# Attention logits and their transposes in two 64-row halves of the array, two quads of heads at a time

## The chip, the cores and the metric

The kernel runs on one core of a Trainium2 chip. The metric is the device time of one execution in microseconds (us); lower is better. Shorthand: PE is TensorE, DVE VectorE, ACT ScalarE, POOL GpSimd, SP SyncE. L476 is line 476 of the kernel.

## The reference

For 16 batches of 128 tokens with 256 features: a layer norm, cross attention with 32 heads of 8 features and axial rotary positions, a residual, a second layer norm, and a mixture of 32 experts (6 per token) with a shared expert. The change is in the attention:

```python
q = (x @ Wq).reshape(b, n, 32, 8)
k, v = jnp.split(ctx @ Wkv, 2, axis=-1)      # each reshaped to (b, ctx_n, 32, 8)
q, k = apply_axial_rope(q, pos), apply_axial_rope(k, pos)
logits = jnp.einsum('bqhd,bkhd->bhqk', q, k) * scale
w = jax.nn.softmax(logits, axis=-1)
attn = jnp.einsum('bhqk,bkhd->bqhd', w, v).reshape(b, n, 256)
x = x + attn @ Wout + bout
```

## The kernel before

Attention runs first, then the mixture. In attention the 32 heads of a batch are 8 quads of 4; each head has a slot of 32 partitions in the array, 24 of them holding its 8 features as fp16 high and low parts, and row 24 (`MAXROW`) the negated row maximum. `qst` is q transposed, [128 slots' rows, quad, 128 tokens]; `kz` is k transposed, spread over four blocks j such that block j is zero outside slot j, [128, 4, quad, 128 keys].

For each quad the logits are computed twice. `logits_q` (L568, matmul L576) computes S for a quad in one matmul of 512 columns (four heads of 128 keys) into `SB[u % 2]`; DVE's `row_max` (L472) reduces it to four maxima per token in `mx` (L476). For every two quads ("half" 0 to 3) PE transposes `mx` into a corner of `SB[1]` (`transpose_max`, L578), DVE copies it to `mxs` (`evac_max`, L479, L483), and SP sends it to row `MAXROW` of `qst` (L295). Then `logits_k` (L582, L589) computes S^T minus the maximum, four matmuls of 128 columns, into `STB[g % 2]`; ACT takes the exponential (L369) into `pw[g % 4]`, in fp32. `weigh_values` (L593, L600) multiplies by V in four column strips of 32 and accumulates in `OB`; one such call is a quad, 8 matmuls in the trace.

SB and STB are two PSUM banks each. S^T of quad g waits for exponential g - 2 (`at_least(pe, exp_ok, QUADS * m.n + g - 1)`), S of quad u for reduction u - 2, and for odd u also for the copy of the maxima (`mxs_ok`). The exponential of quad g waits for `weigh_values` of quad g - 4, since `pw` has four buffers.

The order is written out by hand. Each engine runs `period(b)` for b = -3 to 16 with eight steps g = 0 to 7, and each handles several batches at once: b (the current one), m1 = b + 1, m2, m3, m4 ahead and o = b - 1 behind. All queues are in order. On PE (L626): at each g `logits_k(b, g)`; at odd g `transpose_max`; at each g `logits_q` of quad g + 5 of b (g < 3) or g - 3 of m1. Besides, g = 0: `project_v(m1)` (L566), `weigh_values(o, 4..7)`, `transpose_xc(m3)` (L538, L539); g = 1: `transpose_q(m1)` (L554), `project_k(m3)` (L543); g = 2: `project_q(m3)` (L547); g = 3: `transpose_outputs(o)` (L608); g = 4: `weigh_values(b, 0..3)`, `transpose_attn(o)` (L615); g = 5: `transpose_k(m2)` (L561), which waits for DVE's rotation (L469) to have left its bank; g = 6: `project_out(o)` (L621).

ACT (L363) has the exponential first at each g, and then g = 0: copies to V (L374, which waits for all of `weigh_values(o)`) and xcT (L359); g = 1: qst (L380); g = 2: OT (L407); g = 4: the norm of m4 (L353); g = 5: attnT (L397); g = 6: kT (L402). DVE (L495) has at g = 3 the rotation by cos (`rope_cos`, L462), the copy of maxima (L483), a reduction, and `normalise(o)` (L489 reciprocal, L492 product); at g = 4 a reduction and the rotation by sin (L469, two instructions); at g = 7 the residual (L501), the copy of maxima, a reduction and statistics (L514). SP (L279) sends kT to kz in four DMAs at the start of a period once all exponentials of the batch before are done, and the maxima at odd g. POOL splits q and k into fp16 parts (`split`, L247 to L260) after the rotation.

Of the kernel before, what the change touches and what calls it, by code (L numbers as in the profile page):

```python
# [157 lines left out]
def attention(nc, sem, X, identf, st2, ring, ahead, x, ctx_in, pos, wq, wkv, wout, bout):  # L158
    with ExitStack() as es:
# [181 lines left out]
        def _(act):  # L341
# [21 lines left out]
            def period(b):  # L363
                m1, m2, m3, m4, o = b + 1, b + 2, b + 3, b + 4, b + -1
                for g in range(QUADS):
                    if inside(b):
                        act.wait_ge(st_mm, QUADS * b.n + g + 1)
                        at_least(act, pv_mm, QUADS * b.n + g - 3)
                        act.activation(pw[g % 4][:, :], STB[g % 2][:, :], ACT.Exp, scale=SCALE).then_inc(exp_ok, 1)  # L369
# [7 lines left out]
                    if g == 1 and inside(m1):  # L377
                            at_least(act, qstT_mm, m1.n + 1)
                            at_least(act, st_mm, QUADS * b.n)
# [32 lines left out]
        def _(dve):  # L412
# [59 lines left out]
            def row_max(m, u):  # L472
                dve.wait_ge(s_mm, QUADS * m.n + u + 1)
                if not (isinstance(m.n, int) and 4 * m.n + u // 2 < 2):
                    dve.wait_ge(mxT_mm, 4 * m.n + u // 2 - 1)
                dve.tensor_reduce(mx[u // 2 % 2][:, u % 2:8:2], SB[u % 2][:, :].rearrange("p (j t) -> p j t", j=4),  # L476
                                  axis=AX.X, op=ALU.max, negate=True).then_inc(max_ok, 1)
# [17 lines left out]
            def period(b):  # L495
                m1, m3, o = b + 1, b + 3, b + -1
                for g in range(QUADS):
# [10 lines left out]
                    who, u = (b, g + 5) if g < 3 else (m1, g - 3)  # L508
                    if inside(who):
                        row_max(who, u)  # L510
# [18 lines left out]
        def _(pe):  # L529
# [38 lines left out]
            def logits_q(m, u):  # L568

                if u == 0:  # L570
                    at_least(pe, qst_ok, m.n + 1)
                    pe.wait_ge(kz_in[m.par], 64 * (m.half + 1))
                at_least(pe, max_ok, QUADS * m.n + u - 1)
                if u % 2:
                    at_least(pe, mxs_ok, 4 * m.n + u // 2)
                pe.matmul(SB[u % 2][:, :], qst[m.par][:, u, :], kz[m.par][:, :, u, :], start=True, stop=True).then_inc(s_mm, 1)  # L576
# [5 lines left out]
            def logits_k(m, g):  # L582

                at_least(pe, exp_ok, QUADS * m.n + g - 1)
                if g % 2 == 0:
                    half = g // 2
                    pe.wait_ge(mr_in[half % 2], 16 * (2 * m.n + half // 2 + 1))
                for j in range(4):
                    ins = pe.matmul(STB[g % 2][:, j * P:j * P + P], kz[m.par][:, j, g, :], qst[m.par][:, g, :],  # L589
                                    start=True, stop=True)  # L590
# [710 lines left out]
```

## Time and profile before

| | us |
|---|---|
| median of 3 runs | 429.85 (429.79 to 432.39) |
| the profiled execution, its own time | 428.33 |
| its span, first to last instruction | 426.6 |
| mean granted TensorE clock | 0.911 |
| PE busy | 317.8 (74%) |
| DVE busy | 236.8 (55%) |
| ACT busy | 201.3 (47%) |
| POOL busy | 167.3 (39%) |

Times of instructions come from the one profiled execution. A matmul is in work from its start to its modelled end, and the next one starts before that end; the distance between starts is what a matmul takes of the engine in a stream. Attention runs until about 237 us, the mixture from there.

### The profile page before, as it was taken

To read this page: it belongs to the slowest core of one execution; us is meant where nothing else is said; L and a number is where in the kernel's file an instruction comes from. 1 tells how busy PE (TensorE), PEld (TensorE's weight loads), DVE (VectorE), ACT (ScalarE), POOL (GpSimd) and SP (SyncE) were. 2 spreads that over 40 slices of the span, in tenths; PEclk is the share of its full clock that TensorE was granted. 3 is DMA by queue.
4 is the path that set the end of the run, shared out by engine and by line. 5 is a ranking of instruction groups with operands and counts; after the bars stand their busy time and mean duration, and the time that the engine had idled before them with its cause. 6 is when DMAs were issued, how large, how long until landed. Compare 5 with 4: busy or idle time off the path is not lost. (4 is left out here: it accounts for less than half of the span.)

```text
span 426.6 us, 9168 instructions
## 1 busy us (share of the span) xinstructions
PE 317.8 (74%) x2986; PEld 212.4 (50%) x2986; DVE 236.8 (55%) x624; ACT 201.3 (47%) x378; POOL 167.3 (39%) x241
## 2 busy tenths in 40 slices
PE   0473878999999999999986588797988996775000
PEld 0251646777777777777664234454566543331000
DVE  6464447677777777777774457999682321221000
ACT  2232456776777777776774663535724121110000
POOL 9342144233344444443000200443785225776720
PEclk9997689999999999999999589999999999996555
DMA  7898276211111111103200235110336694222255
GB/s 191 252 256 238 55 211 193 55 35 31 31 32 32 31 32 25 31 23 91 62 18 2 75 125 206 25 51 1 101 102 206 198 245 109 28 26 26 28 94 111
DMA packets 35035, 39.27 MB, mean 92 GB/s; under 512 B 8032, under 2 KB 29120, under 8 KB 34752
## 3 DMA queue, kind: packets, MB, share of 16 engines
q1 hardware_dynamic: 24082, 21.55, 17.6%
q10 hardware_dynamic: 8030, 11.93, 9.7%
q0 software_dynamic: 2896, 5.44, 7.4%
q8 instruction: 15, 0.25, 0.3%
q14 instruction: 12, 0.10, 0.1%
HBM read 26.36 MB, written 10.32 MB: 86 GB/s over the span
## 5 line engine op out<-in xcount | busy, mean ns | idle before, releaser
L476 DVE TENSOR_REDUCE mx<-bank 128x4 f16<-128x512 f32 x128 | 87.2, 684 | 30.0 <-PE bank L576 29.9
L369 ACT ACTIVATE pw<-bank 128x512 f32<-128x512 f32 x128 | 76.8, 601 | 52.0 <-PE bank L600 31.0
L247 POOL TENSOR_TENSOR rot<-t 128x256 f32<-128x256 f32 x30 | 21.1, 726 | 108.1 <-DVE t L469 108.1
L576 PE MATMUL bank<-kz,qst 128*128 128x512 f16 x128 | 51.1, 400 | 7.2 <-DMA kz<-kT 5.9
L589 PE MATMUL bank<-qst,kz 128*128 128x128 f16 x512 | 50.7, 223 | 6.5 <-DMA qst<-mxs 5.9
L589 PEld LDWEIGHTS bank<-qst,kz 128*128 128x128 f16 x512 | 38.3, 100 | 19.4 <-issue 7.5
L600 PE MATMUL bank<-pw,V 128*32 128x128 f32 x1024 | 34.7, 276 | 0.0
L877 POOL DMA_INDIRECT out<-ac,dst x16 | 21.7, 1354 | 28.6 <-DVE ac L1118 10.4
L1118 DVE TENSOR_SCALAR ac<-mbank,wpair 128x256 f32<-128x256 f32 x16 | 7.7, 484 | 44.0 <-DMA odd<-ac,dst 41.2
L1175 PE MATMUL mbank<-hT,WSG 128*128 128x512 f16 (+1 forms) x144 | 32.0, 379 | 0.0
L600 PEld LDWEIGHTS bank<-pw,V 128*32 128x32 f32 x1024 | 25.9, 109 | 8.8 <-issue 7.5
L1187 PE MATMUL mbank<-WSD,ac 128*128 128x256 f32 (+1 forms) x96 | 23.8, 404 | 6.5 <-POOL ac L836 4.0
L836 POOL TENSOR_TENSOR ac<-ac,sg 128x512 f32<-128x512 f32 (+1 forms) x9 | 11.8, 1319 | 39.9 <-ACT ac L917 39.9
L483 DVE COPY mxs<-bank 8x128 f16<-8x128 f16 x64 | 13.1, 205 | 22.4 <-PE bank L580 22.4
L1187 PEld LDWEIGHTS mbank<-WSD,ac 128*128 128x128 f32 (+1 forms) x96 | 19.1, 202 | 11.3 <-POOL ac L836 6.5
L877 POOL DMA_INDIRECT odd<-ac,dst x16 | 21.7, 1354 | 7.4 <-DVE ac L1118 5.3
L402 ACT COPY kT<-bank 128x1024 f16<-128x1024 f16 x16 | 16.1, 1008 | 14.6 <-PE bank L561 12.5
L1175 PEld LDWEIGHTS mbank<-hT,WSG 128*128 128x128 f16 (+1 forms) x144 | 15.1, 106 | 15.4 <-ACT ac L917 0.4
L258 POOL TENSOR_TENSOR tokst<-rot,tokst 128x256 f16<-128x256 f32 x30 | 20.1, 671 | 4.4
L538 PE MATMUL bank<-identf,xn 128*128 128x128 f32 x32 | 7.9, 333 | 15.8 <-ACT xn L353 13.9
L1244 PE MATMUL mbank<-ring_gu,xbT 128*64 128x352 f32 x112 | 18.9, 460 | 0.7 <-ACT xbT L778 0.7
L970 ACT ACTIVATE ac<-mbank 128x176 f32<-128x176 f32 x16 | 5.1, 318 | 29.7 <-PE mbank L1244 29.7
(175 smaller groups left out, 645.9 us busy)
## 6 DMA issues: line engine op xcount, KB each, us to landing
ring_gu<-in_L_ffn_w_gate_up ACTq DMA_DIRECT2D x20, 352.0 KB
kz<-kT SPq DMA_DIRECT2D x64, 64.0 KB, 2.0
ring_dn<-in_L_ffn_w_down ACTq DMA_DIRECT2D x10, 352.0 KB
ring_gu<-in_L_ffn_w_gate_up SPq DMA_DIRECT2D x8, 352.0 KB
X<-in_x SPq DMA_DIRECT2D x4, 512.0 KB, 7.4
table<-ac SPq DMA_DIRECT2D x8, 256.0 KB, 2.1
odd<-zero SPq DMA_DIRECT2D x1, 2048.0 KB, 7.2
out<-X SPq DMA_DIRECT2D x4, 512.0 KB, 3.3
```

The lines of the kernel that those rows point to most:

```text
L247: eng.tensor_tensor(rot[:, part], t1[:, part], t2[:, part], ALU.add).then_inc(rot_ok[w], 1)
L258: eng.tensor_tensor(tokst[m.par][:, w, :, a:a + HD], r, hi, ALU.subtract)
L369: act.activation(pw[g % 4][:, :], STB[g % 2][:, :], ACT.Exp, scale=SCALE).then_inc(exp_ok, 1)
L402: act.copy(kT[:, :, :], M1[:, :].bitcast(F16).rearrange("p (q t) -> p q t", q=QUADS)).then_inc(kT_ok, 1)
L476: dve.tensor_reduce(mx[u // 2 % 2][:, u % 2:8:2], SB[u % 2][:, :].rearrange("p (j t) -> p j t", j=4), axis=AX.X, op=ALU.max, negate=True). ...
L576: pe.matmul(SB[u % 2][:, :], qst[m.par][:, u, :], kz[m.par][:, :, u, :], start=True, stop=True).then_inc(s_mm, 1)
L589: ins = pe.matmul(STB[g % 2][:, j * P:j * P + P], kz[m.par][:, j, g, :], qst[m.par][:, g, :], start=True, stop=True)
L600: ins = pe.matmul(OB[m.par][32 * j:32 * j + 32, (g % 4) * P:(g % 4) * P + P], V[m.par][:, a:a + SLOT], pw[g % 4][:, j * P:j * P + P], star ...
L877: pool.indirect_dma_start(to[:, :], bass.IndirectOffsetOnAxis(ap=dst[:, 2 * k + w:2 * k + w + 1], axis=0), ys[k % 3][rows, :], None, compu ...
L1175: ins = pe.matmul(GU[2 * (i % 2) + w][0:n, :], WSG[:, c, u, w * SHARED + a:w * SHARED + a + n], hT[:, v, c, 512 * k:512 * k + 512], start= ...
L1187: ins = pe.matmul(DN[m % 2][:, 0:D], ac[k % 2][0:n, f, j * P:j * P + P], WSD[0:n, f, :], start=(f == 0), stop=(f == 2))
L1244: ins = pe.matmul(EB[k % 3][lane, 0:2 * INNER], xbT[:, c, e * CAP:e * CAP + LANE], ring.gu[place][:, e % 2, c, :], start=(c == 0), stop=(c ...
```

## The change

S and S^T go by pairs of quads p = 0 to 3. Rows 0 to 63 of the array hold slots 0 and 1 of a quad, rows 64 to 127 slots 2 and 3. The upper half (r = 0) writes `SB[0]` or `STB[0]`, the lower half `SB[1]` or `STB[1]`, each for both quads (a = 0, 1) of the pair. `logits_q(m, p)` is four matmuls of 256 columns on 64 rows in place of two of 512 on 128 rows; `logits_k(m, p)` is eight matmuls of 128 columns on 64 rows in place of eight on 128. `row_max(m, p)` is two reductions, one for each bank; the exponentials are two for each pair as before, one for each bank. A bank pair is written when both of its last readers are done. PE runs `logits_k` and `logits_q` at even g only, and `transpose_max` at the end of odd g.

```diff
--- before.py
+++ after.py
@@ -364,9 +364,10 @@
                 m1, m2, m3, m4, o = b + 1, b + 2, b + 3, b + 4, b + -1
                 for g in range(QUADS):
                     if inside(b):
-                        act.wait_ge(st_mm, QUADS * b.n + g + 1)
-                        at_least(act, pv_mm, QUADS * b.n + g - 3)
-                        act.activation(pw[g % 4][:, :], STB[g % 2][:, :], ACT.Exp, scale=SCALE).then_inc(exp_ok, 1)
+                        r = g % 2
+                        act.wait_ge(st_mm, 4 * b.n + g // 2 + 1)
+                        at_least(act, pv_mm, QUADS * b.n + g - r - 2)
+                        act.activation(pw[g % 4][:, :], STB[r][:, :], ACT.Exp, scale=SCALE).then_inc(exp_ok, 1)
                     if g == 0 and inside(m1):
                         at_least(act, v_mm, m1.n + 1)
                         act.wait_ge(consts, 6)
@@ -376,7 +377,7 @@
                         evac_xcT(m3)
                     if g == 1 and inside(m1):
                             at_least(act, qstT_mm, m1.n + 1)
-                            at_least(act, st_mm, QUADS * b.n)
+                            at_least(act, st_mm, 4 * b.n)
                             act.copy(qst[m1.par][:, :, :], M0[:, :].bitcast(F16).rearrange("p (q t) -> p q t", q=QUADS)).then_inc(qst_ok, 1)
                     if g == 2 and inside(o):
                         evac_OT(o)
@@ -469,12 +470,14 @@
                     ins = dve.tensor_tensor(o2[:, :, :, r], qk[:, :, :, 1 - r], rs, ALU.mult)
                 ins.then_inc(rope_ok, 1)
 
-            def row_max(m, u):
-                dve.wait_ge(s_mm, QUADS * m.n + u + 1)
-                if not (isinstance(m.n, int) and 4 * m.n + u // 2 < 2):
-                    dve.wait_ge(mxT_mm, 4 * m.n + u // 2 - 1)
-                dve.tensor_reduce(mx[u // 2 % 2][:, u % 2:8:2], SB[u % 2][:, :].rearrange("p (j t) -> p j t", j=4),
-                                  axis=AX.X, op=ALU.max, negate=True).then_inc(max_ok, 1)
+            def row_max(m, p):
+                dve.wait_ge(s_mm, 4 * m.n + p + 1)
+                if not (isinstance(m.n, int) and 4 * m.n + p < 2):
+                    dve.wait_ge(mxT_mm, 4 * m.n + p - 1)
+                for r in range(2):
+                    to = mx[p % 2][:, 4 * r:4 * r + 4].rearrange("p (j a) -> p a j", a=2)
+                    dve.tensor_reduce(to, SB[r][:, :].rearrange("p (a j t) -> p a j t", a=2, j=2),
+                                      axis=AX.X, op=ALU.max, negate=True).then_inc(max_ok, 1)
 
             def evac_max(m, half):
                 k = 4 * m.n + half
@@ -505,9 +508,9 @@
                         who, half = (b, (g + 3) // 2) if g < 5 else (m1, (g - 5) // 2)
                         if inside(who):
                             evac_max(who, half)
-                    who, u = (b, g + 5) if g < 3 else (m1, g - 3)
-                    if inside(who):
-                        row_max(who, u)
+                    who, p = (b, g // 2 + 2) if g < 4 else (m1, g // 2 - 2)
+                    if g % 2 == 0 and inside(who):
+                        row_max(who, p)
                     if g == 7 and inside(o):
                         dve.wait_ge(x1_ok, o.n + 1)
                         dve.wait_ge(rope_tab, 3)
@@ -565,40 +568,45 @@
                 at_least(pe, x1_ok, m.n - 2)
                 pe.matmul(M0[:, 0:D], xcT[m.par][:, DK, :], WKV[:, D:2 * D], start=True, stop=True).then_inc(v_mm, 1)
 
-            def logits_q(m, u):
-
-                if u == 0:
+            def logits_q(m, p):
+
+                if p == 0:
                     at_least(pe, qst_ok, m.n + 1)
                     pe.wait_ge(kz_in[m.par], 64 * (m.half + 1))
-                at_least(pe, max_ok, QUADS * m.n + u - 1)
-                if u % 2:
-                    at_least(pe, mxs_ok, 4 * m.n + u // 2)
-                pe.matmul(SB[u % 2][:, :], qst[m.par][:, u, :], kz[m.par][:, :, u, :], start=True, stop=True).then_inc(s_mm, 1)
+                at_least(pe, max_ok, 2 * (4 * m.n + p))
+                at_least(pe, mxs_ok, 4 * m.n + p)
+                for a in range(2):
+                    for r in range(2):
+                        rows = slice(64 * r, 64 * r + 64)
+                        ins = pe.matmul(SB[r][:, a * D:a * D + D], qst[m.par][rows, 2 * p + a, :], kz[m.par][rows, 2 * r:2 * r + 2, 2 * p + a, :],
+                                        start=True, stop=True, tile_position=(64 * r, 0))
+                ins.then_inc(s_mm, 1)
 
             def transpose_max(m, half):
                 pe.wait_ge(max_ok, QUADS * m.n + 2 * half + 2)
                 pe.transpose(SB[1][:, 0:P // 2].bitcast(F16), mx[half % 2][:, :], identh[:, :]).then_inc(mxT_mm, 1)
 
-            def logits_k(m, g):
-
-                at_least(pe, exp_ok, QUADS * m.n + g - 1)
-                if g % 2 == 0:
-                    half = g // 2
-                    pe.wait_ge(mr_in[half % 2], 16 * (2 * m.n + half // 2 + 1))
-                for j in range(4):
-                    ins = pe.matmul(STB[g % 2][:, j * P:j * P + P], kz[m.par][:, j, g, :], qst[m.par][:, g, :],
-                                    start=True, stop=True)
+            def logits_k(m, p):
+
+                at_least(pe, exp_ok, QUADS * m.n + 2 * p)
+                pe.wait_ge(mr_in[p % 2], 16 * (2 * m.n + p // 2 + 1))
+                for a in range(2):
+                    for j in range(2):
+                        for r in range(2):
+                            rows, c = slice(64 * r, 64 * r + 64), (2 * a + j) * P
+                            ins = pe.matmul(STB[r][:, c:c + P], kz[m.par][rows, 2 * r + j, 2 * p + a, :], qst[m.par][rows, 2 * p + a, :],
+                                            start=True, stop=True, tile_position=(64 * r, 0))
                 ins.then_inc(st_mm, 1)
 
             def weigh_values(m, g):
-                pe.wait_ge(exp_ok, QUADS * m.n + g + 1)
+                pe.wait_ge(exp_ok, QUADS * m.n + g // 2 * 2 + 2)
                 if g == 0:
                     at_least(pe, v_ok, m.n + 1)
                     at_least(pe, attn_ok, m.n - 1)
                 for j in range(4):
                     a = (4 * g + j) * SLOT
                     ins = pe.matmul(OB[m.par][32 * j:32 * j + 32, (g % 4) * P:(g % 4) * P + P], V[m.par][:, a:a + SLOT],
-                                    pw[g % 4][:, j * P:j * P + P], start=(g == 0), stop=(g >= 4), tile_position=(0, 32 * j),
+                                    pw[g // 2 % 2 * 2 + j // 2][:, (g % 2 * 2 + j % 2) * P:(g % 2 * 2 + j % 2) * P + P], start=(g == 0), stop=(g >= 4), tile_position=(0, 32 * j),
                                     skip_group_check=True)
                 ins.then_inc(pv_mm, 1)
 
@@ -626,15 +634,11 @@
             def period(b):
                 m1, m2, m3, o = b + 1, b + 2, b + 3, b + -1
                 for g in range(QUADS):
-                    if inside(b):
-                        logits_k(b, g)
-                    if g % 2 == 1:
-                        who, half = (b, (g + 3) // 2) if g < 5 else (m1, (g - 5) // 2)
-                        if inside(who):
-                            transpose_max(who, half)
-                    who, u = (b, g + 5) if g < 3 else (m1, g - 3)
-                    if inside(who):
-                        logits_q(who, u)
+                    if g % 2 == 0 and inside(b):
+                        logits_k(b, g // 2)
+                    who, p = (b, g // 2 + 2) if g < 4 else (m1, g // 2 - 2)
+                    if g % 2 == 0 and inside(who):
+                        logits_q(who, p)
                     if g == 0 and inside(m1):
                         project_v(m1)
                     if g == 0 and inside(o):
@@ -659,6 +663,8 @@
                         transpose_k(m2)
                     if g == 6 and inside(o):
                         project_out(o)
+                    if g % 2 == 1 and inside(who):
+                        transpose_max(who, p)
             periods(pe, period)
```

## Rows read from the trace of the kernel before

**Rows 1.** The page: busy time of each engine; granted clock in 40 slices

```profile
PE 317.8 (74%) x2986; PEld 212.4 (50%) x2986; DVE 236.8 (55%) x624; ACT 201.3 (47%) x378; POOL 167.3 (39%) x241
...
PEclk9997689999999999999999589999999999996555
```

**Rows 2.** Two stretches of attention: length, then busy PE, PEld, DVE, ACT, POOL; clock

```profile
100.00:200.00 100.00, 96.56 (x1253) 74.67 (x1252) 73.63 (x168) 72.93 (x130) 40.97 (x77) 1.00 0.13 33
143.90:155.44 11.54, 11.16 (x157) 8.67 (x149) 8.31 (x20) 8.44 (x15) 4.76 (x10) 1.00 0.12 29
```

**Rows 3.** The matmuls of line 621 between 100 and 200 us

```profile
L621 PE MATMUL bank<-WO,attnT x36: 379/379/379, 106.3 to 198.9; 128*128 128x256 f32 x36
```

**Rows 4.** Who waited for whom between 100 and 200 us: total, times, longest

```profile
ACT pw L369 <- PE bank L600: 18.4, 17, 1.2
...
ACT pw L369 <- PE bank L589: 7.2, 18, 0.6
```

**Rows 5.** Timeline of ACT in one period: start, duration, work

```profile
143.90 0.60 ACT L369 ACTIVATE pw<-bank 128x512 f32<-128x512 f32 x1 [1.14 <-PE bank L600]
...
145.00 0.48 ACT L359 COPY xcT<-bank 128x384 f32<-128x384 f32 x1
...
146.85 0.60 ACT L369 ACTIVATE pw<-bank 128x512 f32<-128x512 f32 x1
147.34 0.59 ACT L407 COPY OT<-bank 128x512 f32<-128x512 f32 x1
147.95 0.60 ACT L369 ACTIVATE pw<-bank 128x512 f32<-128x512 f32 x1
149.67 0.60 ACT L369 ACTIVATE pw<-bank 128x512 f32<-128x512 f32 x1 [1.11 <-PE bank L600]
...
152.40 0.60 ACT L369 ACTIVATE pw<-bank 128x512 f32<-128x512 f32 x1 [0.59 <-PE bank L589]
152.90 1.01 ACT L402 COPY kT<-bank 128x1024 f16<-128x1024 f16 x1
153.79 0.61 ACT L369 ACTIVATE pw<-bank 128x512 f32<-128x512 f32 x1
155.44 0.60 ACT L369 ACTIVATE pw<-bank 128x512 f32<-128x512 f32 x1 [1.04 <-PE bank L600]
```

**Rows 6.** Timeline of PE, the same period

```profile
142.88 0.60 PE L566 MATMUL bank<-WKV,xcT 128*128 128x256 f32 x2
143.40 1.08 PE L600 MATMUL bank<-pw,V 128*32 128x128 f32 x32
144.41 0.44 PE L538 MATMUL bank<-identf,xn 128*128 128x128 f32 x2
...
147.53 0.39 PE L589 MATMUL bank<-qst,kz 128*128 128x128 f16 x4
...
148.06 0.60 PE L608 MATMUL bank<-identf,OT 128*128 128x128 f32 x4
...
151.98 0.39 PE L589 MATMUL bank<-qst,kz 128*128 128x128 f16 x4
152.20 0.38 PE L576 MATMUL bank<-kz,qst 128*128 128x512 f16 x1
152.42 1.03 PE L621 MATMUL bank<-WO,attnT 128*128 128x256 f32 x4
```

**Rows 7.** Timeline of DVE, the same period

```profile
147.93 0.69 DVE L462 TENSOR_TENSOR t<-bank,RC 128x512 f32<-128x512 f32 x1 [0.37 <-PE bank L547]
148.54 0.20 DVE L483 COPY mxs<-bank 8x128 f16<-8x128 f16 x1
...
150.05 0.68 DVE L476 TENSOR_REDUCE mx<-bank 128x4 f16<-128x512 f32 x1
150.64 0.74 DVE L469 TENSOR_TENSOR t<-bank,RS 128x256 f32<-128x256 f32 x2
```

**Rows 8.** Timeline of PE, early

```profile
36.95 1.01 PE L576 MATMUL bank<-kz,qst 128*128 128x512 f16 x2 [5.94 <-DMA kz<-kT]
```

## The prediction

> **What bounds the kernel now.** I read the busy shares first [rows 1]: TensorE (PE) 74%, DVE 55%, ScalarE (ACT) 47%, and the clock line shows full speed through the stage that the diff touches. The diff is all in the attention stage, so I cut out its steady part [rows 2]: in 100 us PE has work in flight for 96.56 us, DVE 73.63, ACT 72.93. One period (one batch of 128 tokens) takes 11.49 us: nine groups of four L621 matmuls, the first at 106.3, the last ending its starts at 198.9, with 0.65 us of starts inside a group, so (198.9 - 0.65 - 106.3)/8 [rows 3]. The code has 12 such full periods (b = 1 to 12) and five thinner ones around them.
>
> The waits [rows 4] say who is late: ACT waits 18.4 us for the weighted sums (L600) in 17 cases, two per period, and 7.2 us for S^T (L589). PE itself hardly waits, so at present PE's column time sets the period, and ACT has 3.1 us of idle time in it (11.54 less 8.44 [rows 2]).
>
> I use ACT's eight exponentials as a clock. Their starts in one period [rows 5] divide 11.54 us into four stretches: A, exponential 0 to 3, 143.90 to 147.95, 4.05; B, 3 to 4, 1.72; C, 4 to 6, 149.67 to 152.40, 2.73; D, 6 to the next 0, 152.40 to 155.44, 3.04.
>
> **What the change does to PE alone.** Per period it keeps 32 S^T matmuls of 128 columns and turns 8 S matmuls of 512 columns into 16 of 256. Four S^T matmuls start within 0.22 us now (151.98 to 152.20), one S takes 0.22 us (152.20 to 152.42) [rows 6]. If the two 64-row halves stream side by side, a block of eight S^T takes 0.22 to 0.23 us instead of 0.44, a block of four S 0.22 instead of 0.43: over the four blocks PE gains about 1.74 us.
>
> Against that stand changes of the array's shape. The only ones now are around the L600 matmuls (128*32): the second L566 starts at 143.09 (0.60 for the two, less the 0.38 of one) and streams to 143.31, L600 starts at 143.40; its 32 matmuls stream to about 144.30, the next one starts at 144.41 [rows 6]. So one change costs about 0.1. Before there are 4 per period, afterwards 11 (four S^T/S blocks in and out, one exit falling together with an entry of L600): +7, or +0.7 us. Below, the cost might be 0 where PE stands waiting anyway; above, 0.17 (the start of the second L538 is also late, 0.06). I take 0.1.
>
> No row shows two row halves at work. The nearest is L600: 32 fp32 matmuls on four column strips start within 0.81 us (1.08 less the 0.27 of the last), so four of them take 0.10 [rows 6]. Four undivided fp32 ones (L608) start 0.11 apart, (0.60 - 0.27)/3, so the four strips take the time of one. That speaks for overlap of tiles; the other end is no overlap at all (0.44 to 0.46 and 0.43 per block), which I keep for a rival. The Trainium skill, TensorE: Matmul & The Clock Gate, Part 3 on packing small matmuls, says that row tiles run at the same time (3.07 times for four of them). By it the sum is my forecast, without it the first rival below; no run here shows it yet.
>
> **What it does to the waits.** Before, S^T has two banks used in turn: S^T of quad g needs only exponential g-2, so PE is one quad ahead of ACT. Afterwards a block of S^T writes both banks and waits for both exponentials of the pair before. ACT and PE then take turns at g = 0, 2, 4, 6. The maxima likewise: S of a pair waits for both reductions of the pair before, their transpose and its copy (L483). And the first exponential after each L600 block waits for two quads of it instead of one. I walk the four stretches again, with latencies from rows: the end of a matmul (151.98 + 0.39) to the exponential behind it (152.40) 0.03 to 0.04, the end of an exponential (146.85 + 0.60) to S^T (147.53) 0.08 [rows 5, 6].
>
> D. Exponential 6, copy to kT after 0.50, exponential 7 after another 0.89, its end after 0.61 [rows 5]. Before, S^T of the next quad 0 was long in its bank. Now it starts 0.08 later, and ahead of exponential 0 PE, in order, has: S^T 0.23, S 0.22, change of shape 0.10, project_v 0.43, change 0.09, and two quads of L600 with their latency, 0.35 + 0.27 + 0.04 = 0.66. Sum 0.50 + 0.89 + 0.61 + 0.08 + 0.23 + 0.22 + 0.10 + 0.43 + 0.09 + 0.66 = 3.81, against 3.04: +0.77.
>
> A. The copies to V and xcT wait for the whole L600 block and the transposes behind it; as exponential 0 itself is 0.2 later in that block, the rest of the wait is 0.2 shorter (xcT starts 0.90 after it instead of 1.10). Exponential 3 needs no S^T of its own any more, and follows the OT copy by 0.50 instead of 0.61 [rows 5]. Sum 4.05 - 0.20 - 0.11 = 3.74: -0.31.
>
> B. Exponential 3 ends after 0.60, S^T starts 0.17 later (a transpose of maxima and the change of shape), takes 0.23. S is not ready: it waits for the copy of the maxima of pair 3. Their S starts some 0.55 us after exponential 1's end (behind S^T, and behind the copy of the maxima of pair 2, which PE transposes only after L543), 1.25 before exponential 3. From there come 0.43 for S itself, two reductions (0.60 + 0.68), L462 0.69, L483 0.20 [rows 7], less overlaps of 0.07 each, and 0.08 back: 1.3 us after exponential 3 starts, 0.30 later than S^T would allow. Then S 0.22, change 0.10, two quads 0.66. Sum 0.60 + 0.17 + 0.23 + 0.30 + 0.22 + 0.10 + 0.66 = 2.28: +0.56. The 0.30 is the least certain term; it can be 0 or 0.6.
>
> C. DVE's queue decides: reciprocal, product, two reductions, then L469, whose end frees the bank for L561 [rows 7]. Before, that end (151.39) was 1.72 after exponential 4; the same work gives 1.7 now. L561, then the moved transpose of maxima (0.06) and a change of shape (0.10) before S^T: 2.73 + 0.16 = 2.89: +0.16.
>
> Sum 3.74 + 2.28 + 2.89 + 3.81 = 12.72, or +1.18 a period. The reductions and exponentials themselves are the same in number and size (a reduction writes its four maxima at another stride). The maxima's DMA to qst is not made late: the copy of pair 2's maxima ends at about 2.4 us after exponential 0, S^T of that pair comes 2.1 us behind it; no landing time for this DMA stands in the rows, and if it took over 2.1 us it would add the excess. On SP it is queued behind the four kz issues, which end before it is due. The two M0/M1 helpers (project_q, transposes, POOL's split) stay hidden: PE now stands idle 1.2 us before L561.
>
> Twelve periods give 14.2. The five thinner ones have fewer helpers to fill the turns with, but less in PE's queue too; I put half of D and B on each, 0.6, together 3.0. The profiled execution took 428.33 (span 426.6); 428.33 + 17.2 = 445.5, and as the median of the runs is 1.5 above the profiled one, 447.0. What comes behind attention starts later by as much and is unchanged.
>
> A second rule belongs here, the Trainium skill, TensorEngine Tiling (Array Packing), on the PSUM bottleneck: tiling speeds up TensorE but not the emptying of PSUM. The trace agrees so far as in one period DVE has 8.31 and ACT 8.44 us of work [rows 2], and the diff takes none of it away.
>
> **Rivals.** (1) The halves don't overlap. Then D grows by another 0.44 (S^T and S), C by 0.23, B by 0.22 and some 0.30 for a DVE chain that starts later: +1.19, in all 2.37 x 12 + 5 = 33, so 463. For it: no row shows row halves. Against: L600's strips overlap.
> (2) Faster. PE's column time is the bound, as it is in flight 96.56 of 100 us, and the turns hide in ACT's 3 us of idle time; then PE's balance counts, -1.74 + 0.7 = -1.04 a period, 12 times: -12.5, so 417. The place is D: it decides if the next exponential 0 comes no later than 3.04 after exponential 6. Against it: exponential 7 now stands ahead of all of PE's work there, and the sum is 3.81.
> (3) Gain and loss cancel: shape changes cost nothing, and the maxima aren't late in B. D is then 3.62 and B 1.88, the period +0.3 to +0.4: 433 to 434.
> (4) The clock. It is 0.50 in the records after PE's first long idle time, 5.94 us before 36.95 [rows 8]. The longest idle piece in my walk is 1.25 us, so I expect full speed; if it fell for good, the streaming that the walk has on the path (1.2 in D, 0.8 in B, 0.75 in C, 0.5 in A) would double: +3.3 a period, 487.
>
> **How the numbers follow.** Forecast 0.55 (438 to 455), rival 1 0.22, rival 4 0.05, rival 2 0.10, rival 3 0.08. Likeliest 447; 433 to 466 leaves out rival 2 and the worst of 1 and 4. Slower by over 1% 0.82, within 1% 0.08 (about what a measurement of this kernel can tell from no change), faster 0.10.
>
> **What would show it.** Right: period 12.5 to 13; ACT's wait before exponential 0 grows to about 1.8 us, before exponential 4 to 1.7; PE gets idle time ahead of S^T put down to ACT L369, and before L561; S^T's eight matmuls start within 0.2 us, in pairs. Wrong: eight starts over 0.4 us (rival 1); PE still in flight 95% with a shorter period (rival 2); a granted clock of 0.5 between 60 and 230 us (rival 4).

## The result, and the profile after

The changed kernel takes 458.75 us (456.85 to 462.14, 4 runs) against 430.27 us for the kernel before: 1.0724 times as long, 95% interval 1.0662 to 1.0785. The profiled execution took 460.24 us, its span is 458.5 (before 426.6): +31.9. The forecast was 447 with 433 to 466.

The page first: busy times and the granted clock, which answer to [rows 1].

```profile
PE 322.3 (70%) x3114; PEld 195.7 (43%) x3114; DVE 236.6 (52%) x624; ACT 196.7 (43%) x378; POOL 167.7 (37%) x241
...
PEclk9995977999999999999988978999899999788555
```

PE's share fell from 74% to 70%. The clock line has 14 digits under 9 instead of 9; in the first third they are as many as before, three, but lower (5, 7, 7 instead of 7, 6, 8). In the changed kernel L370 is the exponential, L479 the reductions, L587 the transpose of the maxima, L486 its copy, L581 S, L597 S^T, L608 the weighted sums, L463 and L470 the rotations, L550 project_q, L564 transpose_k, L569 project_v, L616 transpose_outputs, L629 project_out and L231 the loop over the batches. Next the steady part and one period of it (columns: length, busy PE, PEld, DVE, ACT, POOL, clock), as in [rows 2]:

```profile
100.00:200.00 100.00, 83.91 (x1147) 54.29 (x1143) 64.13 (x144) 60.44 (x112) 37.21 (x70) 1.00 0.10 24
147.91:161.42 13.51, 11.28 (x165) 7.33 (x157) 8.41 (x20) 8.09 (x16) 4.80 (x9) 1.00 0.10 25
```

PE has work in flight for 83.91 us of 100, before 96.56; DVE 64.13, before 73.63. No engine became the bound, each has more idle time. The waits in the same 100 us (total, times, longest), as in [rows 4]:

```profile
ACT pw L370 <- PE bank L608: 33.0, 15, 2.5
DVE mxs L486 <- PE bank L587: 23.0, 15, 2.3
...
ACT pw L370 <- PE bank L597: 6.9, 8, 0.9
PE bank L564 <- DVE t L470: 6.7, 8, 0.9
...
PE bank L581 <- DVE mxs L486: 4.4, 23, 0.2
```

ACT's waits for the weighted sums went from 18.4 to 33.0 us, twice per period as before, and DVE waits 23.0 us for the transposed maxima, before 10.4. PE waits for DVE in return (L564, L581). One period on ACT, PE and DVE; these answer to [rows 5], [rows 6] and [rows 7]. Columns: start, duration, work, idle time before and its releaser.

```profile
147.91 0.60 ACT L370 ACTIVATE pw<-bank 128x512 f32<-128x512 f32 x1 [2.11 <-PE bank L608]
...
151.58 0.65 ACT L370 ACTIVATE pw<-bank 128x512 f32<-128x512 f32 x1
154.27 0.60 ACT L370 ACTIVATE pw<-bank 128x512 f32<-128x512 f32 x1 [2.04 <-PE bank L608]
...
156.93 0.60 ACT L370 ACTIVATE pw<-bank 128x512 f32<-128x512 f32 x1 [0.82 <-PE bank L597]
157.42 1.01 ACT L403 COPY kT<-bank 128x1024 f16<-128x1024 f16 x1
158.31 0.61 ACT L370 ACTIVATE pw<-bank 128x512 f32<-128x512 f32 x1
161.42 0.60 ACT L370 ACTIVATE pw<-bank 128x512 f32<-128x512 f32 x1 [2.49 <-PE bank L608]
```

```profile
150.09 0.40 PE L597 MATMUL bank<-qst,kz 64*128 64x128 f16 x8
150.66 0.39 PE L581 MATMUL bank<-kz,qst 64*128 64x256 f16 x4 [0.17 <-DVE mxs L486]
150.98 1.13 PE L550 MATMUL bank<-WQ,xcT 128*128 128x256 f32 x4
151.95 0.60 PE L616 MATMUL bank<-identf,OT 128*128 128x128 f32 x4
152.43 0.23 PE L587 MATMUL bank<-identh,mx 128*128 128x128 f16 x1
152.60 0.40 PE L597 MATMUL bank<-qst,kz 64*128 64x128 f16 x8
153.24 0.40 PE L581 MATMUL bank<-kz,qst 64*128 64x256 f16 x4 [0.24 <-DVE mxs L486]
153.56 1.08 PE L608 MATMUL bank<-pw,V 128*32 128x128 f32 x32
...
155.80 0.62 PE L564 MATMUL bank<-identh,tokst 128*128 128x128 f16 x8 [0.79 <-DVE t L470]
...
158.76 0.23 PE L587 MATMUL bank<-identh,mx 128*128 128x128 f16 x1 [0.32 <-DVE mx L479]
159.34 0.46 PE L597 MATMUL bank<-qst,kz 64*128 64x128 f16 x8 [0.35 <-ACT pw L370]
159.75 0.40 PE L581 MATMUL bank<-kz,qst 64*128 64x256 f16 x4
160.08 0.70 PE L569 MATMUL bank<-WKV,xcT 128*128 128x256 f32 x2
160.71 1.08 PE L608 MATMUL bank<-pw,V 128*32 128x128 f32 x32
```

```profile
150.30 0.21 DVE L486 COPY mxs<-bank 8x128 f16<-8x128 f16 x1 [2.33 <-PE bank L587]
151.09 1.29 DVE L479 TENSOR_REDUCE mx<-bank 128x4 f16<-128x512 f32 x2 [0.58 <-PE bank L581]
152.29 0.68 DVE L463 TENSOR_TENSOR t<-bank,RC 128x512 f32<-128x512 f32 x1
152.89 0.20 DVE L486 COPY mxs<-bank 8x128 f16<-8x128 f16 x1
...
156.62 0.21 DVE L486 COPY mxs<-bank 8x128 f16<-8x128 f16 x1 [0.87 <-PE bank L587]
```

The halves do run side by side: the last start of eight S^T matmuls (L597) is 0.18 us after the first (0.40 less the 0.22 of one), before it was 0.17 for four [rows 6]. The stretches are here A 3.67, B 151.58 to 154.27 = 2.69, C 2.66, D 156.93 to 161.42 = 4.49.

To compare runs I take the mean of each stretch over batches 4 to 11, from the starts of the exponentials (us):

| kernel | median | period | A | B | C | D |
|---|---|---|---|---|---|---|
| before | 430.27 | 11.52 | 4.06 | 1.67 | 2.70 | 3.10 |
| forecast | 447.0 | 12.72 | 3.74 | 2.28 | 2.89 | 3.81 |
| changed | 458.75 | 13.32 | 3.63 | 2.74 | 2.69 | 4.26 |
| whole_array | 464.72 | 13.97 | 3.65 | 3.13 | 2.77 | 4.43 |
| st_pairs_only | 442.29 | 12.41 | 3.63 | 2.26 | 2.59 | 3.93 |
| s_pairs_only | 453.49 | 13.30 | 4.64 | 1.79 | 2.66 | 4.21 |
| spread | 464.53 | 14.03 | 4.99 | 2.05 | 3.99 | 3.00 |
| half_max_changed | 448.84 | 12.61 | 3.63 | 2.71 | 2.17 | 4.10 |
| half_max_before | 422.51 | 10.96 | 4.06 | 1.67 | 2.16 | 3.07 |
| maxima_first | 449.65 | 12.89 | 3.63 | 2.40 | 2.80 | 4.06 |
| copy_first | 456.48 | 13.34 | 3.63 | 2.40 | 3.19 | 4.13 |
| copy_sin_first | 457.76 | 13.48 | 3.63 | 2.39 | 3.33 | 4.13 |
| before_spread | 442.92 | 12.56 | 5.56 | 0.93 | 3.43 | 2.64 |
| before_sin_first | 432.34 | 11.80 | 4.06 | 1.67 | 2.97 | 3.10 |
| before_turned | 428.37 | 11.48 | 4.06 | 1.67 | 2.30 | 3.46 |

### The profile page after: what moved, and what is told of

Its sections match the earlier page's. It is cut to its first block and busy times, and to the rows that moved or that the text cites. A ratio compares the mean times of both kernels' runs of the same rounds, so it can differ in the third digit from the quotient of the medians.

```text
span 458.5 us, 9222 instructions
## 1 busy us (share of the span) xinstructions
PE 322.3 (70%) x3114; PEld 195.7 (43%) x3114; DVE 236.6 (52%) x624; ACT 196.7 (43%) x378; POOL 167.7 (37%) x241
## 5 line engine op out<-in xcount | busy, mean ns | idle before, releaser
L370 ACT ACTIVATE pw<-bank 128x512 f32<-128x512 f32 x128 | 76.9, 608 | 88.4 <-PE bank L608 71.2
L479 DVE TENSOR_REDUCE mx<-bank 128x4 f16<-128x512 f32 x128 | 82.4, 685 | 38.2 <-PE bank L581 38.2
L486 DVE COPY mxs<-bank 8x128 f16<-8x128 f16 x64 | 13.4, 210 | 53.8 <-PE bank L587 53.8
L608 PE MATMUL bank<-pw,V 128*32 128x128 f32 x1024 | 37.5, 291 | 0.0
L581 PE MATMUL bank<-kz,qst 64*128 64x256 f16 x256 | 26.8, 285 | 12.1 <-DVE mxs L486 6.7
L597 PE MATMUL bank<-qst,kz 64*128 64x128 f16 x512 | 26.8, 225 | 11.9 <-DMA qst<-mxs 6.0
L608 PEld LDWEIGHTS bank<-pw,V 128*32 128x32 f32 x1024 | 28.1, 116 | 9.8 <-issue 9.1
L883 POOL DMA_INDIRECT out<-ac,dst x16 | 21.7, 1355 | 27.6 <-DVE ac L1124 10.4
L1193 PE MATMUL mbank<-WSD,ac 128*128 128x256 f32 (+1 forms) x96 | 22.1, 382 | 6.3 <-POOL ac L842 4.0
L597 PEld LDWEIGHTS bank<-qst,kz 64*128 64x128 f16 x512 | 15.3, 96 | 21.8 <-issue 10.6
L1250 PE MATMUL mbank<-ring_gu,xbT 128*64 128x352 f32 x112 | 21.0, 503 | 0.7 <-ACT xbT L784 0.7
L564 PE MATMUL bank<-identh,tokst 128*128 128x128 f16 x128 | 10.6, 230 | 14.8 <-DVE t L470 14.8
L587 PE MATMUL bank<-identh,mx 128*128 128x128 f16 x64 | 14.8, 231 | 7.7 <-DVE mx L479 7.7
```

Source lines behind the costliest of these rows:

```text
L370: act.activation(pw[g % 4][:, :], STB[r][:, :], ACT.Exp, scale=SCALE).then_inc(exp_ok, 1)
L479: dve.tensor_reduce(to, SB[r][:, :].rearrange("p (a j t) -> p a j t", a=2, j=2), axis=AX.X, op=ALU.max, negate=True).then_inc(max_ok, 1)
L581: ins = pe.matmul(SB[r][:, a * D:a * D + D], qst[m.par][rows, 2 * p + a, :], kz[m.par][rows, 2 * r:2 * r + 2, 2 * p + a, :], start=True, s ...
L597: ins = pe.matmul(STB[r][:, c:c + P], kz[m.par][rows, 2 * r + j, 2 * p + a, :], qst[m.par][rows, 2 * p + a, :], start=True, stop=True, til ...
L608: ins = pe.matmul(OB[m.par][32 * j:32 * j + 32, (g % 4) * P:(g % 4) * P + P], V[m.par][:, a:a + SLOT], pw[g // 2 % 2 * 2 + j // 2][:, (g % ...
L883: pool.indirect_dma_start(to[:, :], bass.IndirectOffsetOnAxis(ap=dst[:, 2 * k + w:2 * k + w + 1], axis=0), ys[k % 3][rows, :], None, compu ...
```

## The experiments

**whole_array** gives the row halves back and keeps everything else.

```diff
-                        rows = slice(64 * r, 64 * r + 64)
+                        rows = slice(0, P)
...
-                                        start=True, stop=True, tile_position=(64 * r, 0))
+                                        start=True, stop=True)
```

(the same in `logits_k`)

> The changed kernel with the two row halves taken away: the same instructions, banks, waits and order, but each S and S^T matmul on all 128 rows (kz is zero outside a slot, so the values are the same). Theory 1, the turns cost the time (both banks are waited for, ACT and PE stop for one another): the loss stays, and the column time that the halves save comes on top, 0.23 for a block of S^T and 0.22 for one of S where they are on the path, less some 0.1 to 0.2 for each change of shape that goes away: 455 to 468 us, period 13.2 to 14.2. Theory 2, the seven more changes of the array's shape cost the time: they are all gone here, so it falls to 435 to 447 us, period under 12.3.

464.72 us, 1.0873 times before (1.0756 to 1.0989); period 13.97. Theory 2 is out as the main cause: without any of the new changes of shape the kernel is slower still. The pairing alone, on an undivided array and with the transpose of the maxima at its new place, costs 13.97 - 11.52 = 2.45 us a period; the row halves give back 0.65 of it (D 0.17, B 0.39, C 0.08).

**st_pairs_only** and **s_pairs_only** make one half of the change each. The first keeps the old `logits_q`, `row_max`, `transpose_max` and their order, the second the old `logits_k`, exponential and `pw` layout.

Of PE's order, in st_pairs_only:

```python
                    if g % 2 == 0 and inside(b):
                        logits_k(b, g // 2)
...
                    if inside(who):
                        logits_q(who, u)
```

and in s_pairs_only:

```python
                    if inside(b):
                        logits_k(b, g)
...
                    if g % 2 == 0 and inside(who):
                        logits_q(who, p)
```

> Only S^T and the exponentials go by pairs in row halves; S, the reductions and the copies of the maxima are those of the kernel before. Theory 1: the turn between exponential 7 and the next exponential 0 stays, so stretch D stays near 3.8 to 4.4 us, while B falls back towards 2.0: 440 to 452 us. Theory 1b, the maxima's chain is what makes the kernel late: 430 to 436 us. Theory 2 (changes of shape, as many as in the changed kernel): 450 to 458 us.

442.29 us, 1.0372 (1.0256 to 1.0487): as theory 1 has it, with D at 3.93.

> Only S and the reductions go by pairs in row halves; S^T and the exponentials alternate between two banks as before. Theory 1: D is near 3.0 to 3.3 again, B keeps part of its growth (S waits for the copy of the maxima): 432 to 444 us. Theory 1b, the maxima's chain carries the loss: 446 to 458 us. Theory 2: 450 to 458 us.

453.49 us, 1.0639 (1.0514 to 1.0764): theory 1b. Theory 1 wanted 432 to 444 and D near 3.2; D is 4.21 with S^T alternating as before. So the turn of the maxima (S, two reductions, transpose, copy, next S) is the dearer of the two, +1.78 a period by itself against +0.89 for S^T, and together they cost no more than it does (+1.80). s_pairs_only also has the transpose of the maxima at its new place, st_pairs_only the old one. That the two are chains through the same in-order queue, of which the longer counts, fits these numbers; no run shows it by itself.

**spread** and **before_spread** issue the weighted sums two quads at a time, in the changed kernel and in the one before.

```diff
-                    if g == 0 and inside(o):
-                        for q in range(4, QUADS):
-                            weigh_values(o, q)
-                    if g == 4 and inside(b):
-                        for q in range(4):
-                            weigh_values(b, q)
+                    if g % 2 == 0:
+                        late, q = (o, QUADS) if g == 0 else (b, g)
+                        if inside(late):
+                            weigh_values(late, q - 2)
+                            weigh_values(late, q - 1)
```

> The changed kernel with the weighted sums issued two quads at a time at g = 0, 2, 4, 6, each two steps after their exponentials, instead of four at g = 0 and four at g = 4. Exponentials 0 and 4 then no longer wait for two quads of L608 issued behind S^T, S and project_v. Theory 1: D falls from about 4.3 to 2.6 to 3.0 and B from 2.7 to about 2.0, period 11.3 to 12.3, 433 to 446 us. Theory 2: two more changes of shape in each period (13 instead of 11), slower than the changed kernel, 460 to 464 us.

464.53 us, 1.0864 (1.0746 to 1.0981). Both stretches it was aimed at fell as theory 1 said, D to 3.00 and B to 2.05, and A and C grew by more (4.99, 3.99). In the 100 us ACT's wait for S^T (L597) grew from 6.9 to 31.7 us, and the one for the weighted sums is gone. That is the mark of a wait that only changes its place: exponentials 0 and 4 come early, and the next S^T comes late. Its steady part is not all at full clock either (0.97 from 100 to 200 us, 0.72 from 160 to 166), which is in these numbers.

> The kernel before with the weighted sums issued two quads at a time at g = 0, 2, 4, 6. ACT's waits for L600 (18.4 us in 100) mostly go. If PE's column time is the bound before, the four more changes of shape in each period cost more than that: period 11.7 to 12.2, 432 to 439 us. If ACT's waits were the bound: 420 to 427 us.

442.92 us, 1.0374 (1.0287 to 1.0461), period +1.04, slower than both readings. PE has work in flight for 93.72 of 100 us, before 96.56, so of the 1.04 some 0.64 is work in flight, 0.16 for each of the four more changes of shape, and the rest is idle time: 4.0 us in the 100 before `transpose_attn` (L615), which waits for DVE's product (L492), a wait that the kernel before hardly has. The first reading gave the direction; the wait was not in it.

**half_max_changed** and **half_max_before** shorten the reductions: the maximum is taken over half the keys.

```diff
-                    dve.tensor_reduce(to, SB[r][:, :].rearrange("p (a j t) -> p a j t", a=2, j=2),
+                    dve.tensor_reduce(to, SB[r][:, :].rearrange("p (a j t) -> p a j t", a=2, j=2)[:, :, :, 0:P // 2],
```

> The changed kernel with each reduction over half the keys (64 of 128 per head), so each of the eight reductions of a period is some 0.27 us shorter; the rest is untouched (softmax is the same for any offset). Theory 1b, the chain S, two reductions, transpose, copy, next S sets the period: each of four turns gets up to 0.5 us shorter where nothing else in PE's queue is later, period 13.3 to 11.8 to 12.6, 438 to 450 us. Theory 1, the turns between PE and the exponentials alone set it, the reductions are beside: period over 13.0, 455 to 460 us.

448.84 us, 1.0425 (1.0341 to 1.0508), period 13.32 to 12.61. DVE's time is on the path, as 1b says, but only for 0.71 us of the 2.1 taken away: 0.52 of it in C, 0.16 in D, 0.03 in B. DVE's timeline of this run shows why B did not move:

```profile
149.45 0.76 DVE L479 TENSOR_REDUCE mx<-bank 128x4 f16<-128x256 f32 x2 [0.58 <-PE bank L581]
150.62 0.69 DVE L463 TENSOR_TENSOR t<-bank,RC 128x512 f32<-128x512 f32 x1 [0.41 <-PE bank L550]
151.23 0.20 DVE L486 COPY mxs<-bank 8x128 f16<-8x128 f16 x1
```

The two reductions now take 0.76 us in place of 1.29, but the copy of the maxima (L486) is queued behind the rotation by cos (L463), and that waits for project_q (L550) on PE.

> The same shortening of the reductions in the kernel before. If PE's column time sets the period there, as the prediction says, nothing is gained: period 11.3 to 11.5, 427 to 431 us. If DVE's chain had been the bound before as well, the period falls by 0.5 us or more, 420 to 424 us.

422.51 us (416.13 to 424.5), 0.9765 (0.9671 to 0.9859), a miss: the prediction's "PE's column time sets the period" does not hold in C, which fell by 0.54; A and B did not move and D hardly did (3.10 to 3.07). In C DVE's reductions and rotation held up L561 all along. The trace before has it, 2.2 us in 100, in nine cases; in the period of [rows 6]:

```profile
151.53 0.61 PE L561 MATMUL bank<-identh,tokst 128*128 128x128 f16 x8 [0.28 <-DVE t L469]
```

**maxima_first** moves `transpose_max` to the beginning of its step; **copy_first** also swaps `rope_cos` and `evac_max` on DVE; **copy_sin_first** also puts `rope_sin` ahead of `row_max` at g = 4.

```diff
+                    if g % 2 == 1 and inside(who):
+                        transpose_max(who, p)
                     if g % 2 == 0 and inside(who):
                         logits_q(who, p)
...
-                    if g % 2 == 1 and inside(who):
-                        transpose_max(who, p)
```

> The changed kernel with the transpose of the maxima at the beginning of g = 1, 3, 5, 7 (as in the kernel before) instead of at the end. Theory 1b: the first turn is then not held up by transpose_q and project_k (some 1 us of it), the maxima of pair 0 of the next batch leave 0.4 to 0.7 us earlier, so S^T at g = 0 doesn't wait for their DMA: period 12.6 to 13.1, 448 to 456 us. Theory 1: no change, 456 to 460 us.

449.65 us, 1.0462 (1.0401 to 1.0524): some 9 us of the loss was only where the transpose stood. In the profiled executions 3.2 us of the gain lie in the first two periods (28.8 instead of 32.0) and 5.3 in the ten after them. In D the S^T block at g = 0 then starts 0.13 us after exponential 7 in every period, while in the changed kernel it was 0.41 in every other one. The copy of those maxima now ends 3.2 us ahead of it instead of 2.2 to 2.5.

> The changed kernel with the transpose of the maxima first in its step, and at g = 3 the copy of the maxima (L486) ahead of the rotation by cos, which waits for project_q. Theory 1b (S waits for the copy, and the copy for other work queued ahead of it): S of the next pair starts 0.3 to 0.4 us earlier in B, B 2.0 to 2.1 instead of 2.40, period 12.4 to 12.7, 442 to 447 us. If B is set by exponential 3 and S^T alone: as maxima_first, 448 to 451 us.

456.48 us (450.6 to 459.38, the profiled one 454.55; no interval on the ratio), period 13.34, a miss. B stayed at 2.40. With the transpose first, PE waits there for the reductions (0.33 us before L587), transpose_outputs follows it, and S^T stands behind both: the copy of the maxima is done before S^T starts and does not set B. C grew from 2.80 to 3.19. DVE, with the copy ahead of the rotation by cos, stands idle until the transpose has come:

```profile
150.41 0.21 DVE L486 COPY mxs<-bank 8x128 f16<-8x128 f16 x1 [0.33 <-PE bank L587]
150.71 0.69 DVE L463 TENSOR_TENSOR t<-bank,RC 128x512 f32<-128x512 f32 x1
```

In maxima_first the rotation starts 0.09 us before the end of the reductions, here 0.62 behind it (149.41 + 0.68 to 150.71), and the normalising, the reductions and L470, for which L564 waits, stand behind it in DVE's queue.

> As copy_first, and the rotation by sin ahead of the pair's reductions at g = 4. L564 starts up to 1.2 us earlier; what then ends last in C is the reductions of that pair, their transpose and copy, on which the next S waits but not S^T: C 2.2 to 2.5 instead of 2.80, period 12.0 to 12.4, 437 to 444 us. Were the turns harmless and only the order at fault, it would come down to the kernel before, 428 to 432 us.

457.76 us, 1.0745 (1.0665 to 1.0825), a miss: with the transpose of the maxima first at g = 5, L564 stands behind it in PE's queue and so behind the reductions that now come after the rotation.

**before_sin_first** and **before_turned** use the finding on C in the kernel before; the second also puts, at g = 5, `transpose_k` ahead of `transpose_max` (the lines at their old places go).

```diff
+                    if g == 4 and inside(m3):
+                        rope_sin(m3)
                     who, u = (b, g + 5) if g < 3 else (m1, g - 3)
                     if inside(who):
                         row_max(who, u)
...
-                        if inside(who):
+                        if g != 5 and inside(who):
                             transpose_max(who, half)
...
+                    if g == 5 and inside(m1):
+                        transpose_max(m1, 0)
```

> The kernel before with one change of DVE's order: at g = 4 the rotation by sin (L469) stands ahead of the reduction instead of behind it. If stretch C is bound by DVE in the kernel before, as the shorter reductions suggest (they took 0.54 us out of C alone), L561 starts some 0.4 to 0.6 us earlier and C falls from 2.70 to about 2.2 to 2.4: 422 to 426 us. If PE's column time alone sets the period: no change, 428 to 431 us. The reduction is then later by 0.74 us, and if the chain of the maxima takes it on, up to 432 us.

432.34 us, 1.0147 (1.0085 to 1.021): slower, C 2.97, for the same reason as above: `transpose_max` (L580) stands ahead of L561, and PE waits before it for the reduction, 4.8 us in 100, in nine cases.

> The kernel before with the rotation by sin ahead of the reduction on DVE (g = 4) and, on PE at g = 5, S of the next quad and transpose_k (L561) ahead of the transpose of the maxima, which had held L561 behind the later reduction in before_sin_first. If stretch C is bound by the rotation's end and by nothing else, L561 starts without PE's idle time of 0.4 to 0.5 us and C falls from 2.70 to 2.2 to 2.4: period 11.0 to 11.3, 422 to 426 us. If the maxima's chain (copy, then S of the quad after, then its reduction) takes the gain back in D: period 11.4 to 11.7, 427 to 432 us.

428.37 us, 0.9974 (0.994 to 1.0009): no difference that can be told. C fell to 2.30 as wanted, and D rose to 3.46. ACT and PE of this run:

```profile
153.19 0.60 ACT L369 ACTIVATE pw<-bank 128x512 f32<-128x512 f32 x1
...
154.81 0.60 ACT L369 ACTIVATE pw<-bank 128x512 f32<-128x512 f32 x1
156.55 0.60 ACT L369 ACTIVATE pw<-bank 128x512 f32<-128x512 f32 x1 [1.14 <-PE bank L600]
```

```profile
152.19 0.61 PE L561 MATMUL bank<-identh,tokst 128*128 128x128 f16 x8
...
153.30 0.39 PE L576 MATMUL bank<-kz,qst 128*128 128x512 f16 x1
153.53 1.03 PE L621 MATMUL bank<-WO,attnT 128*128 128x256 f32 x4
154.39 0.39 PE L589 MATMUL bank<-qst,kz 128*128 128x128 f16 x4
```

L561 has no idle time before it any more, but S (L576, 153.30) now waits for its copy, L621 and S^T of quad 7 (154.39) follow it, and exponential 7 starts 1.62 after exponential 6 instead of 1.39 [rows 5]. No exact version was found that beats the kernel before; the only faster one takes its maxima over half the keys.

## Why the prediction was right or wrong

**The sign and the mechanism were right.** The two banks of a pair are waited for together, and PE, ACT and DVE stop for one another: the idle time grows on all three, ACT waits 2.1 to 2.5 us before exponential 0 and 2.0 to 2.1 before exponential 4 (forecast 1.8 and 1.7), and S^T at g = 0 stands behind exponential 7. The undivided run (+2.45 a period) shows that this and not the tiling costs the time.

**The size was in range partly by luck.** 458.75 lies inside 433 to 466 but outside 438 to 455, which was the forecast itself, and the period is 13.32 where 12.5 to 13 was to show that it was right. The range reached up to 466 to hold rival 1, halves that don't overlap, and that is not what happened.

**Row halves overlap**: 0.18 us of starts for eight against 0.17 for four, so rival 1 is out, though the time came near its 463 by another way. The Trainium skill's statement on row tiles (TensorE: Matmul & The Clock Gate, Part 3) holds here.

**The size was too small**, 17.2 against 31.9 in the profiled executions; the terms below add 7.2, 4.6, 0.9 and 2.0 to it.

- The twelve full periods were given 14.2 us and cost 26.0 (from the starts of exponential 0 of batches 1 and 13: 166.1 against 140.1). The ten from batch 3 on cost 19.0, 1.90 each instead of 1.18: +7.2. The first two cost 7.0 instead of 2.4: +4.6.
- The five thinner ones were given 3.0 and cost 3.9 (attention ends at 267.2 instead of 237.3, 29.9 later, less 26.0): about right. The mixture took 2.0 more, which I had put at nothing; it runs the same instructions, and its granted clock has other stretches at half speed than before. How much of the 2.0 they explain is not shown.

**The step that failed within a period** is what PE does in a turn: its prices, and the moved transpose of the maxima. D was summed to 3.81 and came to 4.49 in the period shown, to 4.11 in the ones between, 4.26 in the mean. Up to the end of exponential 7 it was right (0.49 + 0.89 + 0.61 = 1.99, forecast 2.00). The rest of the period shown, beside maxima_first, where nothing on this way waits for the transpose:

```profile
142.73 0.40 PE L597 MATMUL bank<-qst,kz 64*128 64x128 f16 x8 [0.42 <-ACT pw L370]
142.96 0.39 PE L581 MATMUL bank<-kz,qst 64*128 64x256 f16 x4
143.28 0.70 PE L569 MATMUL bank<-WKV,xcT 128*128 128x256 f32 x2
```

| step of D | forecast | maxima_first | changed, period shown |
|---|---|---|---|
| end of exponential 7 to S^T | 0.08 | 0.13 | 0.42 |
| S^T to S | 0.23 | 0.23 | 0.41 |
| S to project_v | 0.32 | 0.32 | 0.33 |
| project_v to L608 | 0.52 | 0.63 | 0.63 |
| L608 to exponential 0 | 0.66 | 0.71 | 0.71 |

So some 0.2 of the 0.45 that D lacked are prices: half of it is the first fp32 matmul behind a change of shape, which takes 0.10 more (four matmuls of 256 columns, L550, in 1.13 instead of L621's 1.03 [rows 6]); I had seen it once, as 0.06, and left it out. The other 0.24 go with the place of the transpose. In every second period the end of the loop over the batches stands between the transpose and S^T in PE's sequencer, which here reaches it only when the transpose is on its way:

```profile
L231 PEldq COMPARE_BRANCH  x1: 213/213/213, 158.8 to 158.8; - x1
L231 PEldq FUSED_REGOPS  x1: 59/59/59, 159.1 to 159.1; - x1
```

Exponential 7 had ended at 158.92. The periods in which S^T comes 0.4 late are the ones with these rows, and only they. With the transpose at the head of its step (maxima_first) the sequencer passes the same point before exponential 7 has ended, and the delay is gone. In the periods between, S starts 0.32 behind S^T: its copy ends only just before, and S comes 0.15 behind that end, as it does at 150.66 (150.30 + 0.21, then 0.15).

**What the halves were to give back.** The change of shape was put at 0.1. Measured: the last S matmul starts 0.12 after the first (0.39 less 0.27) and the next line 0.20 behind it (142.96 + 0.12 to 143.28), where 256 columns take 0.11, so 0.09 to leave; S^T starts 0.15 to 0.17 behind a transpose that takes 0.06 (152.43 to 152.60), so 0.1 to enter. A block of S^T and S that waits for nothing thus takes 0.18 + 0.05 + 0.12 + 0.20 = 0.55, and 0.2 for entry and first load beside it, where two quads took 0.87 before; where L608 follows there is no such load, 0.65 in place of 0.97. Over the four blocks that is some 0.7 us a period, not 1.04, and the undivided run has 0.65. So rival 2's gain was about two thirds of what I gave it, and the waits took more than all of it. The Trainium skill says that a change of tiling mode drains TensorE (TensorEngine Tiling (Array Packing), Key Properties); the 0.09 to 0.10 at each change agree with it.

**What the sum had wrong besides.** PE was not the bound in C: it waited for DVE's rotation there (half_max_before). And rival 3's own terms add up to 3.74 + 1.88 + 2.79 + 3.62 = 12.03, which is +0.49 a period and not +0.3 to +0.4.

**B** was put at 2.28 and measured 2.69: exponential 3 itself 0.65, to S^T 0.37 (forecast 0.17, since transpose_outputs and the transpose of maxima stand ahead of it), to S 0.64 (forecast 0.53, with the wait for the copy 0.24 in the profile), to L608 0.32, to exponential 4 0.71. I had called the copy the least certain term; maxima_first shows 0.34 of B hanging on where the transpose stands. **A** (3.63 for 3.74) and **C** (2.69 for 2.89) were a little better than said.

**The DMA of the maxima** I had put at under 2.1 us and left out, and between 100 and 200 us this held. The trace's semaphore records have its last arrival 1.6 to 1.7 us after the end of the copy, each time; in the period shown that is 158.44, half a microsecond before exponential 7 ends. So it is not what delays S^T at g = 0. In the early part, while weights of the mixture are loaded, the same records have up to 5.65 us.

**The early part.** There S^T of batch 1 waited for that DMA outright. The timeline of PE and two windows (columns as above), the second window of the kernel before:

```profile
73.82 0.40 PE L597 MATMUL bank<-qst,kz 64*128 64x128 f16 x8 [2.30 <-DMA qst<-mxs]
74.04 0.40 PE L581 MATMUL bank<-kz,qst 64*128 64x256 f16 x4
74.36 1.68 PE L629 MATMUL bank<-WO,attnT 128*128 128x256 f32 x4
```

```profile
57.00:83.00 26.00, 19.53 (x213) 12.75 (x214) 10.30 (x23) 11.71 (x22) 7.26 (x15) 0.74 0.54 149
```

```profile
57.00:83.00 26.00, 23.16 (x291) 17.18 (x291) 16.51 (x36) 17.29 (x30) 7.44 (x14) 0.94 0.52 153
```

Idle 2.30 us, then S^T, S, and four L629 in 1.68 us, where they take 1.13 at full clock. The mean clock of the stretch is 0.74, before 0.94. The kernel before waits for this DMA too (4.0 us in five cases between 55 and 90 us, the longest 2.2), so the wait alone does not set the two apart; the half speed behind it lasted longer. Rival 4, which I had given one chance in twenty for the whole stage and argued away by a longest idle piece of 1.25 us, thus came true for a part of it: the walk was made in the steady part and told nothing of batches 1 and 2. That the idle time brought the clock down is not shown, and how the 4.6 us divide between waits and clock stays open.

## What to carry to other kernels

Before two buffers used in turn are merged into one written at once, write down who waits for both and what stands behind him in each in-order queue, the end of a loop included: here that cost 2.45 us a period, of which about 0.4 hung on where one transpose stood, and the doubled matmul rate gave back 0.65. Count each change of the array's shape on both sides, with the first weight load behind it. And when a stretch is shortened, look at the sum of all stretches: in three of these runs (spread, before_spread, before_turned) the time only moved to another one.

## What I had not expected of the hardware

A pair of row halves starts at most 9 ns apart (234 of the 256 pairs of S^T), and a 64-row S follows the last 64-row S^T by 0.05 us when nothing is waited for (maxima_first), so to stay in the tiled shape costs nothing. Leaving or entering a tiled shape costs 0.09 to 0.10 us, and 0.10 more where an fp32 matmul comes first. The end of a loop took PE's sequencer 0.4 us (158.75 to 159.17), and the profile puts the idle time that it makes down to ACT. Four more changes of shape per period came with 0.64 us more work in flight per period in the kernel before (before_spread), 0.16 each, somewhat more than these rates give; the order of the waits changed there too, so that this is not settled.
